# A two-layer mixture kernel on one core: six gathers, the x loads and low-rank A put later, the router in column halves

## The reference

```python
# layer 0
w = L0_cond_weight[ids]                       # one 1024 x 1024 adapter per sequence
c = einsum('bsi,boi->bso', x, w)
logits = c @ W_router.T                       # 8 experts, the best 2 of the softmax are mixed
h = einsum('td,erd->ter', c, lora_A)          # rank 16 for each expert
lora_out = einsum('ter,eor,te->to', h, lora_B, mix) * 2.0
x1 = x + c @ W_base.T + b_base + lora_out
# layer 1
y = einsum('bct,bcd->bdt', x1, W1[ids])       # a 64 x 64 matrix per sequence, over the tokens
t = y[:, perm] in 16 heads of 64
t = gelu(einsum('bhd,hdm->bhm', t, up))       # 64 -> 256 per head
t = einsum('bhm,hmd->bhd', t, down)           # 256 -> 64
out = x1 + t[:, unperm]
```

## Time and profile before

| what | value |
|---|---|
| median of 3 runs | 652.75 us (651.33 to 653.18) |
| the profiled execution | 651.0 us, its span 649.1 us |
| TensorE matmuls busy | 621.0 us (96% of the span) |
| VectorE, ScalarE, GpSimd busy | 423.4, 141.6, 130.7 us |
| bytes read from and written to HBM | 93.89 and 8.39 MB |

### The profile page before, as it was taken

How to read it: one execution, slowest core, us unless ns; L and a number is a source line. 1 busy time by engine, 2 the same in 40 slices (tenths; PEclk the granted TensorE clock), 3 DMA queues, 4 the chain that set the end, 5 groups by cost and what they waited for, 6 DMA issues and landing times.

```text
span 649.1 us, 10832 instructions
## 1 busy us (share of the span) xinstructions
PE 621.0 (96%) x3146; PEld 356.4 (55%) x3147; DVE 423.4 (65%) x1194; ACT 141.6 (22%) x262; POOL 130.7 (20%) x194
## 2 busy tenths in 40 slices
PE   3899999999999999988999999999999999999995
PEld 3334434444444443456676666767676767676762
DVE  2045666666666666697857795767876769766651
ACT  2200000000000000253423432324332326232323
POOL 5000000111111110060022223131223121322212
PEclk9799999999999999999999999999999999999998
DMA  8999772177778686830022222222222222222221
GB/s 282 411 406 361 261 260 99 45 255 280 312 253 339 250 342 242 346 93 11 17 68 84 69 82 65 82 68 85 65 81 67 83 72 77 73 74 82 66 72 58
DMA packets 42299, 102.87 MB, mean 158 GB/s; under 512 B 8322, under 2 KB 17538, under 8 KB 42242
## 3 DMA queue, kind: packets, MB, share of 16 engines
q1 hardware_dynamic: 34370, 80.24, 34.0%
q0 software_dynamic: 6784, 21.51, 10.1%
q10 hardware_dynamic: 1088, 0.56, 0.3%
HBM read 93.89 MB, written 8.39 MB: 158 GB/s over the span
## 4 chain that ended last, share of the span: by engine, by line
PE 76%; issue 7%; SPq 6%; DMA 5%; DVE 4%; ACT 0%; DVEq 0%; POOL 0%; POOLq 0%; ACTq 0%
PE wide L425 21%; PE bank L507 18%; PE bank L558 9%; PE bank L512 8%; PE wide L548 8%; DMA ring<-adapters_dram 5%; PE bank L535 5%; PE bank L439 3%; SPq L229 3%; SPq L242 2%; PE bank L520 1%; PE bank L521 1%; PE bank L522 1%; DVE c_pair L793 1%; DVE c_lo L903 1%
## 5 line engine op out<-in xcount | busy, mean ns | idle before, releaser
L425 PE MATMUL wide<-ring,x_in 128*64 128x512 f32 x1024 | 227.7, 598 | 5.2 <-DMA ring<-adapters_dram 4.9
L425 PEld LDWEIGHTS wide<-ring,x_in 128*64 128x64 f32 x1024 | 73.6, 137 | 143.9 <-issue 140.3
L939 DVE STREAM_TRANSPOSE x_tok<-xres 32x128 f32<-32x128 f32 x480 | 145.3, 303 | 7.2
L793 DVE STREAM_TRANSPOSE c_pair<-wide 32x256 f32<-32x256 f32 x240 | 107.0, 446 | 61.3 <-issue 34.1
L507 PE MATMUL bank<-c_hi,base_t 128*128 128x512 f32 x512 | 143.9, 403 | 0.0
L507 PEld LDWEIGHTS bank<-c_hi,base_t 128*128 128x128 f32 x512 | 91.5, 188 | 26.9 <-issue 10.8
L680 ACT ACTIVATE act_sb<-wide 128x512 f32<-128x512 f32 x128 | 66.1, 604 | 125.4 <-PE wide L548 125.4
L512 PE MATMUL bank<-c_lo,base_t 128*128 (+1 forms) x256 | 79.2, 390 | 0.5 <-DVE c_lo L903 0.5
L378 POOL DMA_INDIRECT out_dram<-xres,row_out x32 | 35.8, 1119 | 199.2 <-DVE xres L931 199.2
L356 POOL COPY c_all<-c_pair 128x512 f32 x30 | 19.3, 670 | 229.1 <-DVE c_pair L793 229.1
L558 PE MATMUL bank<-act_sb,down_sb 128*64 128x512 f32 x256 | 63.0, 614 | 0.6 <-ACT act_sb L680 0.6
(11 more groups left out here) (101 smaller groups left out, 437.1 us busy)
## 6 DMA issues: line engine op xcount, KB each, us to landing
ring<-adapters_dram SPq DMA_DIRECT2D x120, 512.0 KB, 7.3
x_in<-x_seq_dram SPq DMA_DIRECT2D x32, 256.0 KB
up_raw<-up_dram SPq DMA_DIRECT2D x64, 64.0 KB
down_sb<-down_dram SPq DMA_DIRECT2D x32, 128.0 KB
ar_sb<-lora_a_router_dram ACTq DMA_DIRECT2D x1, 544.0 KB
mix_sb<-mix_dram SPq DMA_DIRECT2D x32, 16.0 KB
xres<-xT_dram,row_in POOLq DMA_INDIRECT x32, 3.5
out_dram<-xres,row_out POOLq DMA_INDIRECT x32, 2.8
```

Source lines behind the costliest of these rows:

```text
L425: last = pe.matmul(acc[half][h][z * TOK:(z + 1) * TOK, :], x_in[:, half, z, k, :], ring[:, k, z, h * HALF:(h + 1) * HALF], start=(k == 0), ...
L793: last = nc.vector.transpose(c_pair[r * SQ:(r + 1) * SQ, :, q * SQ:(q + 1) * SQ], wide[half][q * SQ:(q + 1) * SQ, :, :] .rearrange("p h (k ...
L939: last = nc.vector.transpose(x1_tok[q * SQ:(q + 1) * SQ, :].rearrange("p (c f) -> p c f", f=P)[:, :, f * SQ:(f + 1) * SQ], xres[f * SQ:(f ...
```

## The change

Five things change.

1. Only the gathers of slices 0 and 1 of the base stay at the start (`BASE_FIRST`). Gather 2 + t is issued by GpSimd after it has kept pair t, for t from 0 to 5, and slice j is turned by TensorE in pair j after the router, for j from 2 to 7.
2. The x loads go from SP's queue to ScalarE's. Those of pair 1, and after them the load of `ar_sb`, are issued when block 3 of pair 0 is done; those of pair t + 2 when pair t is done.
3. `router` and `turn_hw` use two matmuls in place of one, each with 64 columns of the array. `turn_hw` is now a product with the identity and no longer a transpose.
4. At the end of stage one the rest of slice 5 is made by GpSimd, ahead of its first four residual fetches, and VectorE's list is in another order: one `base_rest` ahead of the copy out of the accumulator in place of two, and `b_lo` after the last pair's copies.
5. In stage two SP waits in another order for `up` and `down`, and in the last step ScalarE's `x1_tokens` and `up_leading` stand ahead of two of the four gelus.

The diff (left out are the new semaphore `pool_split_ok` and lines that only repeat this):

```diff
--- before.py
+++ after.py
@@ -54,7 +54,9 @@
 CS = KT // 2
-SPLIT_ORDER = (0, 1, 4, 2, 3, 5, 6, 7)
+BASE_FIRST = 2
+SPLIT_ORDER = (0, 1, 4, 2, 3, 6, 7)
+POOL_SPLIT = 5
 GATHERS = range(PAIRS // 4, PAIRS // 4 + KT)
@@ -228,13 +231,8 @@
-            def load_pair(t, half):
-
-                for z in range(2):
-                    seq = of_order(2, t, z, SEQS - 1)
-                    sp.dma_start(x_in[:, half, z, :, :],
-                                 x_seq[bass.ds(seq, 1), :, :, :].rearrange("a p k t -> p (a k) t")) \
-                        .then_inc(x_in_in[half], 16)
+            def load_pair(t):
+
                 which = [of_order(1, t, z, IDS - 1) for z in range(2)]
@@ -261,13 +259,11 @@
-            load_pair(0, 0)
-            load_pair(1, 1)
+            load_pair(0)
+            load_pair(1)
             with sp.Fori(1, PAIRS // 2) as i:
-                for half in range(2):
-
-                    sp.wait_ge(block_done, (i * 2 + half - 1) * KT)
-                    load_pair(i * 2 + half, half)
+                load_pair(i * 2)
+                load_pair(i * 2 + 1)
@@ -296,22 +292,26 @@
...
+            def step(g, j):
+
+                g1, j1 = g + (j + 1) // STEPS, (j + 1) % STEPS
+                last = isinstance(g, int) and g == GROUPS - 1
+                sp.wait_ge(up_ok, g * STEPS + j + 1)
+                load_up(j1)
+                if 2 <= j < 2 + GP and not last:
+                    if j == 2:
+                        sp.wait_ge(y_done, g * STEPS + 1)
+                    load_mix(g + 1, j - 2)
+                sp.wait_ge(d_done, g * STEPS + j)
+                load_down(j1)
+
+            sp.wait_ge(up_ok, 1)
+            load_up(1)
+                for j in range(1, STEPS + 1):
+                    step(g + j // STEPS, j % STEPS)
+            for j in range(1, STEPS - 1):
+                step(GROUPS - 1, j)
@@ -344,8 +344,12 @@
             pool.wait_ge(perm_in, 16)
-            for j in range(KT):
+            def gather_base(j):
                 gather(base_rows[:, j, :, :].rearrange("p k o -> p (k o)"), w_base, perm_sb[:, j:j + 1], base_in[j])
+
+            for j in range(BASE_FIRST):
+                gather_base(j)
+
             def keep_pair(t):
@@ -359,10 +363,16 @@
                 keep_pair(t)
+                if BASE_FIRST + t < KT:
+                    gather_base(BASE_FIRST + t)
                 if t in GATHERS:
...
                     gather(bias[:, j:j + 1], bias_rows, perm_sb[:, j:j + 1], bias_in)
+            pool.wait_ge(base_hi_ok, POOL_SPLIT + 1)
+            on_its_own()
+            pool.tensor_tensor(base_t[:, POOL_SPLIT, 1, :, :], base_rows[:, POOL_SPLIT, :, :],
+                               base_t[:, POOL_SPLIT, 0, :, :].bitcast(F32), ALU.subtract).then_inc(pool_split_ok, 1)
             pool.wait_ge(rows_ok, 2)
@@ -436,28 +446,36 @@
                 for k in range(KT):
-                    last = pe.matmul(router_ps[:, 0:AR], c_pair[:, k, :], ar_sb[:, k, :],
-                                     start=(k == 0), stop=(k == KT - 1))
+                    for z in range(2):
+                        toks = slice(z * TOK, (z + 1) * TOK)
+                        last = pe.matmul(router_ps[toks, 0:AR], c_pair[:, k, toks], ar_sb[:, k, :],
+                                         start=(k == 0), stop=(k == KT - 1), skip_group_check=True)
                 last.then_inc(router_done, 1)
...
                 pe.wait_ge(hw_ok, t + 1)
-                pe.transpose(hw_ps[:, 0:P], hw[:, :], ident[:, :]).then_inc(hw_tr_done, 1)
+                for z in range(2):
+                    half = slice(z * ER // 2, (z + 1) * ER // 2)
+                    last = pe.matmul(hw_ps[half, 0:P], hw[:, half], ident[:, :], start=True, stop=True,
+                                     skip_group_check=True)
+                last.then_inc(hw_tr_done, 1)
...
                 pe.wait_ge(base_in[j], 16)
-                if j >= 2:
-                    pe.wait_ge(base_turned, j - 1)
-                transposes(base_ps[j % 2], [base_rows[:, j, k, :] for k in range(KT)], base_tr)
-
-            def pair(i, half):
+                if j >= BASE_FIRST:
+                    pe.wait_ge(base_turned, j)
+                transposes(base_ps[j if j < BASE_FIRST else 0], [base_rows[:, j, k, :] for k in range(KT)], base_tr)
+
+            def pair(i, half, turns=None):
...
                 router(t - 1)
+                if turns is not None:
+                    turn_base(turns)
                 adapter_blocks(i, half, range(5, 8), landed)
@@ -465,20 +483,19 @@
-            for j in range(KT // 2):
+            for j in range(BASE_FIRST):
                 turn_base(j)
-            for k in range(KT // 2):
-                adapter_blocks(0, 0, [k], (16, 16))
-                turn_base(KT // 2 + k)
-            adapter_blocks(0, 0, range(KT // 2, KT), (16, 16))
+            adapter_blocks(0, 0, range(KT), (16, 16))
             pe.wait_ge(loads_ok, 1)
-            pe.wait_ge(base_turned, KT)
+            pe.wait_ge(base_turned, BASE_FIRST)
             pe.wait_ge(ar_in, 16)
...
             adapter_blocks(0, 1, range(5, 8), landed)
-            with pe.Fori(1, PAIRS // 2 - 1) as i:
+            for j in range(BASE_FIRST, KT):
+                pair((j + 2 - BASE_FIRST) // 2, (j + 2 - BASE_FIRST) % 2, j)
+            with pe.Fori(1 + (KT - BASE_FIRST) // 2, PAIRS // 2 - 1) as i:
                 pair(i, 0)
@@ -640,14 +657,43 @@
-            for j in range(KT):
+            def load_x(t, half):
+
+                for z in range(2):
+                    seq = act.value_load(order[0:1, 2, bass.ds(t + z * PAIRS, 1)], min_val=0, max_val=SEQS - 1)
+                    act.dma_start(x_in[:, half, z, :, :],
+                                  x_seq[bass.ds(seq, 1), :, :, :].rearrange("a p k t -> p (a k) t")) \
+                        .then_inc(x_in_in[half], 16)
+
+            def next_x(t, half):
+                act.wait_ge(block_done, (t + 1) * KT)
+                load_x(t + 2, half)
+
+            def keep_base(j):
                 act.wait_ge(base_tr, j + 1)
...
                     last = nc.scalar.copy(base_rows[:, j, h * KT // 2:(h + 1) * KT // 2, :],
-                                          base_ps[j % 2][h][:, :].rearrange("p (k o) -> p k o", o=P))
+                                          base_ps[j if j < BASE_FIRST else 0][h][:, :]
+                                          .rearrange("p (k o) -> p k o", o=P))
                 last.then_inc(base_turned, 1)
-            with act.Fori(0, PAIRS - 2) as t:
+
+            act.wait_ge(order_ok, 1)
+            load_x(0, 0)
+            for j in range(BASE_FIRST):
+                keep_base(j)
+
+            act.wait_ge(block_done, 4)
+            load_x(1, 1)
+            act.dma_start(ar_sb[:, :, :], lora_a_router.rearrange("(k p) e -> p k e", p=P)).then_inc(ar_in, 16)
+            for t in range(2 + KT - BASE_FIRST):
+                next_x(t, t % 2)
                 tanh(t)
+                if 1 <= t <= KT - BASE_FIRST:
+                    keep_base(BASE_FIRST + t - 1)
+            with act.Fori(1 + (KT - BASE_FIRST) // 2, PAIRS // 2 - 1) as i:
+                for half in range(2):
+                    next_x(i * 2 + half, half)
+                    tanh(i * 2 + half)
             for j in range(0, 5):
@@ -719,12 +765,17 @@
                     c_leading(g + 1, CS - 1)
-                for i in range(4):
-                    gelu(g1, j1, i)
-                up_leading(g, j)
+                gelu(g1, j1, 0)
+                gelu(g1, j1, 1)
+                if isinstance(g, int) and g == GROUPS - 1 and j == STEPS - 1:
+                    x1_tokens(1)
+                    up_leading(g, j)
+                gelu(g1, j1, 2)
+                gelu(g1, j1, 3)
+                if not (isinstance(g, int) and g == GROUPS - 1 and j == STEPS - 1):
+                    up_leading(g, j)
             over_steps(act, step)
-            x1_tokens(1)
             y_leading(GROUPS - 1, STEPS - 1)
@@ -880,20 +931,19 @@
             route(PAIRS - 2)
-            for j in SPLIT_ORDER[3:5]:
-                base_rest(j)
+            base_rest(SPLIT_ORDER[3])
             seqs = last_seqs(dve)
             out_of_acc(PAIRS - 1, 1)
+            base_rest(SPLIT_ORDER[4])
+            turned(PAIRS - 1)
+            keep_last(1, seqs)
+            hw_turned(PAIRS - 2)
             dve.wait_ge(b_hi_ok, 1)
...
             last.then_inc(b_ok, 1)
-            turned(PAIRS - 1)
-            keep_last(1, seqs)
-            hw_turned(PAIRS - 2)
-            base_rest(SPLIT_ORDER[5])
             dve.wait_ge(bias_in, KT * 16)
```

More of the change, by code:

```diff
@@ L178, in build @@
             sem(n) for n in ("b_tr", "b_hi_ok", "b_ok", "base_tr", "base_turned", "base_hi_ok", "base_ok"))
+        pool_split_ok = sem("pool_split_ok")
         block_done, c_tok_ok, turn_done, c_pair_ok, c_kept, last_kept = (
@@ L297, in _ @@
             sp.wait_ge(mix_cleared, 1)
[L299 to L310, removed]
+            def step(g, j):
```

(15 more changed lines are left out.)

## The result

The changed kernel takes 655.38 us (median of 5 runs, 654.75 to 656.66), the kernel before 652.75 (5 runs, 651.33 to 653.18). The ratio is 1.0045, with a 95% interval of 1.0029 to 1.0061: 0.45% slower. Forecast were 642.9 us, in a range that ended at 649.0. The profiled execution took 654.75 us with a span of 652.9, so its span is 3.8 us longer than that of before.

A forecast was written before the change was run, and what follows sets the result against it. TensorE fills stage two, so only stage one, the seam and the last 17 us could move. Terms -7.3 + 7.0 - 3.3 - 2.5 - 0.9 - 2.9 = -9.9 took 652.75 to 642.9 us, range 639.8 to 649.0.

The forecast's parts named there:

- step 1: Start of stage one: six gathers gone, x and low-rank A on ScalarE's queue, so pair 1 starts sooner; -7.3 us.
- the front: Stretch before pair 1, bound by full DMAs; forecast 7.3 us shorter, bounds 5.0 and 8.2.
- the six turns: Base turns moved into pairs 2 to 7, where TensorE has no gap: 1.16 us each, +7.0 us.
- the stalls: TensorE's waits for late ring slots from pair 8 on; all go once SP issues no x loads, -2.5 us.
- the halves: Router and turn in column halves keep one array shape through a pair: 0.22 us less in 15 pairs, -3.3 us.
- the tail: Last step of stage two: mixing begins 1.4 us sooner and the clock stays at 2.4 GHz; -2.9 us.
- the seam: Between the stages: VectorE's copy out of the accumulator begins after one rest, not two; -0.9 us reaches TensorE.
- A: As a rival (elsewhere low-rank A): router halves don't run side by side, router 3.7 us, time 671 us; 7%.
- B: Rival: x and gathers delay ring slots, TensorE waits about 0.8 us in each of five pairs; 646.9 us, 13%.
- C: Rival: the array shape costs nothing, so the column halves give nothing; 646.2 us, 12%.
- D: Rival: front gains only 5.0, tail stays at the low clock, half of the slot stalls stay; 648.1 us, 6%.

The follow-up runs named there:

- e3: Changed kernel with low-rank A and router laid out in DRAM as one 4352-byte row per partition, not eight of 544: 645.56 us against 651.28, ratio 0.9907.
- e10: e1 with the `ar_sb` load issued ahead of x1 on ScalarE's queue, rows still 544 bytes: 652.95 us, one execution.
- e2: Changed kernel with the `ar_sb` load issued first on ScalarE's queue, TensorE's wait left in place: 642.69 us against 651.28, ratio 0.9870.
- e9: e8 with six gathers and their turns moved as in the change, `ar_sb` first, x1 issued after block 3 of pair 0: 643.01 us against 652.45, ratio 0.9861.
- e8: Kernel before plus x on ScalarE's queue, column halves and the new tail order; gathers and seam unchanged: 644.00 us (ratio 0.9883), again 644.18 (0.9879).
- e4: e1 with the seam of the kernel before (slice 5's rest on VectorE, two rests ahead of the copy): 644.66 us against 651.28, ratio 0.9894.
- e1: Changed kernel with TensorE's wait on `ar_in` moved from ahead of pair 1 to ahead of router(0): 644.52 us against 651.28, ratio 0.9896.

## Why the prediction was wrong

**The step that failed is step 1.** It said that by the turn-taking of the queues "x0, x1 and A are safe, and it is pair 1's slots that pay". A was not safe. The Trainium skill, "DMA: Bandwidth & Descriptors", section "Queues, rings and completion order", says turns are taken by the packet; I read a share of the bytes into it. The runs agree so far that turns do not go by bytes: A is made of rows an eighth as long as a ring row, and by e3 and e10 it pays about one ring row for each. The second half of the fault was in my own evidence: I named `ar_sb` among the bytes ahead of pair 1, and not the wait on `ar_in` there, nor what was queued behind it, all of pair 1. A wait that had cost nothing while its load was first became the end of the front. The order of the program and the diff showed both the late issue and the wait; the load's 17.7 us no row of before could show. The front, forecast at -7.3, came out at +5.25. The load's place cost 12.2 us to pair 1's router (56.58 against 44.43 in e2): 9.1 idle, 2.1 at the low clock, 1 for later slots in pair 0.

**Sizes.** With `ar_sb` out of the way the front gains 6.9 (51.33 to 44.43 in e2, forecast 7.3; the 7.6 of e9 are against e8, whose front is 0.5 later than that of before), the six turns cost 7.0 (7.0), the stalls give 2.6 (2.5), the halves 0.20 a pair, 3.0 in all (0.22, 3.3), the tail 3.1 (2.9), the seam nothing (0.9). That makes -8.6 us, 1.3% of 652.75, and e2 measured 1.3%; the forecast was -9.9, 1.5%. So the other terms were sound, and the front would have been too but for one load.

**The seam** (forecast -0.9) gave nothing, in the profile and in e4. This is a second, small fault. The failed point is "the second rest (1.18) fits into the time in which TensorE turns": it took 2.35 beside GpSimd. I had priced GpSimd's subtract in GpSimd's time alone.

**Rivals.** A is out: 32 matmuls with 32 weight loads take 1.85 us, 0.058 us for each pair of instructions. B had late loads, but of the wrong kind and in the wrong place: TensorE waited for slots only in pair 0, never in pairs 1 to 5. C is out by 15.8. Of D neither the low clock in the tail nor the left-over stalls came, and the front came out far worse than its -5.0. No rival had TensorE wait for a load that is not on the ring, and so only 7% were left for slower.

What stays open: whether six gathers are better late. e9 is 0.2% faster than e8 with overlapping intervals.

## What to carry to other kernels

When a load moves to a later place or another queue, find every wait on its semaphore and move it to the first use; the wait that was free is the one to look at. A load of short rows next to a full queue of long ones pays by the row: issue it while the queues are empty, or lay it out in long rows. Work moved out of a transfer-bound stretch has its full price in the compute-bound one: here 7.6 against 7.0.

## What the runs showed of the hardware

- 0.56 MB in rows of 544 bytes took 15.3 to 19.1 us beside a full queue of 4096-byte rows (e10, the changed kernel, e1), 4.1 us at the start of the program (e2), and 9.3 us in rows of 4352 bytes beside the full queue (e3).
- VectorE's subtract of 128 x 1024 took 2.35 us beside a GpSimd subtract and 1.18 without (e1, e4), and ended 1.08 us after GpSimd's, which took 2.73. A copy of 128 x 512 beside it took 0.69 us, as long as without.
- In the tail TensorE's granted clock was still 1.00 after 0.67 us without a matmul, and in the kernel before 0.50 after 2.11 us without one. At the end of stage one e8 had 1.00 in one execution and 0.50 in another, at the same place and after the same gap of 0.78.
- 32 matmuls of 64 columns with their 32 weight loads took 1.85 us, 0.058 us for each pair of instructions.
